# Attention two groups ahead of the routing in a gated mixture-of-experts kernel

## The reference, cut to what matters

```python
# x, ctx: 64 x 64 x 128 (4096 tokens of 128), float32
def _L0_xattn_ref(Q, K):
    scores = jnp.einsum('btd,bsd->bts', K, K)
    mask = jnp.tril(jnp.ones((Lq, Lq), dtype=scores.dtype))
    scores = scores * mask[None, :, :]
    return Q + jnp.einsum('bts,bsd->btd', scores, Q)

def _L0_ffn_ref(x, shared_w1, shared_w2, experts_w1, experts_w2, gate_w):
    shared = jnp.einsum('td,dh->th', x_flat, shared_w1.T)
    shared = jnp.einsum('th,hd->td', jax.nn.silu(shared), shared_w2.T)
    gate_logits = x_flat @ gate_w.T
    top_k_gates, top_k_idx = jax.lax.top_k(gate_logits, TOP_K)   # 2 of 8
    top_k_gates = jax.nn.softmax(top_k_gates, axis=1)
    ...
    h = jnp.einsum('td,ehd->teh', x_flat, experts_w1)            # hidden 512
    expert_out = jnp.einsum('teh,edh->ted', jax.nn.silu(h), experts_w2)
    selected = jnp.einsum('ted,te->td', expert_out, gates)
    return (shared + selected).reshape(B, S, D)

x = x + jnp.tanh(g_xattn[0]) * _L0_xattn_ref(_layernorm(x, axis=-1), ctx_1024)
x = x + jnp.tanh(g_ffn[0]) * _L0_ffn_ref(_layernorm(x, axis=-1), ...)
```

## Time and profile before

| | us |
|---|---|
| median of 3 runs | 280.01 |
| lowest, highest | 279.14, 280.99 |
| the profiled execution | 277.21 |
| its span in the profile | 275.5 |
| TensorE busy | 242.3 (88%) |
| VectorE, ScalarE, POOL busy | 127.1, 132.8, 160.1 |
| chain that ended last: TensorE, VectorE | 70%, 16% |

### The profile page before, as it was taken

The page is one execution under the profiler, slowest core; times in us unless marked ns, Lnnn a source line. Parts: engine busy times, 40 slices in busy tenths (PEclk is TensorE's granted clock), DMA queues, the critical chain, the costliest instruction groups (busy, mean ns, idle before and its releaser), DMA issues.

```text
span 275.5 us, 6308 instructions
## 1 busy us (share of the span) xinstructions
PE 242.3 (88%) x1800; PEld 213.6 (78%) x1805; DVE 127.1 (46%) x576; ACT 132.8 (48%) x293; POOL 160.1 (58%) x209
## 2 busy tenths in 40 slices
PE   8779759799799899988968799999999999999920
PEld 4466347668578577788968799999999999999920
DVE  2957969587887668811222022222110011137303
ACT  1572361637365544425543455555555655555610
POOL 5673877786764368877662465454554545555540
PEclk9977979789999999999999999999999999999985
DMA  6992111111110011775666777777776766899818
GB/s 205 399 385 78 44 51 40 48 43 39 50 42 20 20 43 45 228 183 141 193 185 176 226 221 225 203 217 221 215 217 190 234 209 201 240 272 384 337 50 295
DMA packets 32625, 46.94 MB, mean 170 GB/s; under 512 B 5472, under 2 KB 16480, under 8 KB 32336
## 3 DMA queue, kind: packets, MB, share of 16 engines
q1 hardware_dynamic: 27264, 35.45, 42.7%
q0 software_dynamic: 4320, 8.99, 9.3%
q10 hardware_dynamic: 1008, 2.10, 2.1%
HBM read 34.43 MB, written 12.09 MB: 169 GB/s over the span
## 4 chain that ended last, share of the span: by engine, by line
PE 70%; DVE 16%; issue 5%; ACT 3%; POOL 3%; DMA 2%; SPq 0%; POOLq 0%; DVEq 0%
PE bank L933 24%; PE bank L942 22%; PE bank L875 6%; PE bank L867 5%; PE bank L816 3%; PE bank L917 3%; ACT n L490 3%; PE bank L882 3%; DVE stats L570 2%; PE bank L842 2%; DMA nT<-y_rows 1%; DVE scores L605 1%; PE bank L833 1%; DVE top_at L634 1%; POOL rstd L378 1%
## 5 line engine op out<-in xcount | busy, mean ns | idle before, releaser
L452 POOL DMA_INDIRECT y_rows<-y,dest x71 | 68.9, 970 | 63.9 <-ACT y L546 59.1
L420 POOL DMA_INDIRECT expert_rows<-n,slot x64 | 63.4, 991 | 34.2 <-DVE slot L674 11.2
L933 PE MATMUL bank<-xT,w_ring 128*128 128x128 f32 x568 | 75.5, 276 | 6.5 <-issue 4.9
L933 PEld LDWEIGHTS bank<-xT,w_ring 128*128 128x128 f32 x568 | 69.0, 192 | 7.6 <-issue 5.6
L942 PE MATMUL bank<-w,hT 128*128 x568 | 74.7, 275 | 0.0
L942 PEld LDWEIGHTS bank<-w,hT 128*128 128x128 f32 x568 | 69.0, 192 | 0.0
L540 ACT ACTIVATE hT<-bank 128x512 f32<-128x512 f32 x71 | 42.4, 598 | 43.3 <-PE bank L933 42.9
L774 DVE COPY xT<-bank 128x512 f32<-128x512 f32 (+1 forms) x18 | 12.3, 684 | 101.1 <-PE bank L917 101.1
L875 PEld LDWEIGHTS bank<-sw,sT 128*128 128x128 f32 x256 | 33.3, 195 | 11.1 <-issue 11.1
L546 ACT ACTIVATE y<-bank,gate 128x128 f32<-128x128 f32 x71 | 26.1, 368 | 21.5 <-PE bank L942 21.5
L875 PE MATMUL bank<-sw,sT 128*128 128x128 f32 x256 | 34.3, 280 | 0.0
(11 more groups left out here) (124 smaller groups left out, 223.6 us busy)
## 6 DMA issues: line engine op xcount, KB each, us to landing
w_ring<-in_w1T SPq DMA_DIRECT2D x71, 256.0 KB, 3.4
x_ring<-expert_rows SPq DMA_DIRECT2D x71, 66.0 KB, 3.1
w<-in_w2T SPq DMA_DIRECT2D x2, 1024.0 KB, 15.5
kT<-y_rows SPq DMA_DIRECT2D x8, 256.0 KB, 6.3
nT<-y_rows SPq DMA_DIRECT2D x8, 256.0 KB, 4.1
out<-xres SPq DMA_DIRECT2D x8, 256.0 KB
xres<-in_xP SPq DMA_DIRECT2D x3, 512.0 KB, 10.8
kT<-in_ctxT ACTq DMA_DIRECT2D x3, 512.0 KB, 11.1
```

The lines of the kernel that those rows point to most:

```text
L420: pool.indirect_dma_start(out=x_dram[:, :], out_offset=bass.IndirectOffsetOnAxis(ap=slot[:, i, k:k + 1], axis=0), in_=n[:, i, :], in_offse ...
L452: pool.indirect_dma_start(out=y_dram[:, :], out_offset=bass.IndirectOffsetOnAxis(ap=dest[:, b:b + 1], axis=0), in_=y[:, j], in_offset=None ...
L933: last = pe.matmul(ps_up[b % UP_SLOTS][:, cols], w1_ring[:, b % W_RING, cols], xT[:, s % X_SETS, i * P:(i + 1) * P], start=True, stop=True)
```

## The change

Five things are altered.

1. *Loads.* ScalarE's queue issues only the context of groups 0 and 1. SP issues x of groups 0 and 1, waits until the latter has landed, and then issues x and context of the other groups together, with the shared weights between.
2. *Attention order.* Attention runs two to three groups ahead: in step s TensorE does `score(s+3)`, and `apply_scores(s+2)` after the logits (even s) or at the step's head (odd s). There are fewer `keep_warm` matmuls (8, 3 and 5 in place of 8, 5, 6 and 10). Units are dealt to steps by the table `UNTIL`.
3. *Roots.* `norms` works on two slots at once, in odd steps only: first and second norms of two groups in one run of 13 instructions.
4. *Logits* are read by `max` and `max_index` from PSUM, without the copy to SBUF.
5. *POOL* does a `pause()` after each of the first 40 block scatters.

```diff
-    PER_STEP = 7
+    UNTIL = (7, 14, 20, 27, 33, 40, 46, 52)
...
         def units_of(step):
-            return range((step - 1) * PER_STEP, min(UNITS * (GROUPS + 1), step * PER_STEP)) if step < GROUPS \
-                else range((GROUPS - 1) * PER_STEP, UNITS * (GROUPS + 1))
+            return range(UNTIL[step - 1] if step else 0, UNTIL[step])
...
         def _(sp):
             for i, (a, b) in enumerate(LOADS):
+                if i == 2:
+                    sp.wait_ge(x_in[1], 16)
                 sp.dma_start(xres[:, a * GW:b * GW], xP[:, a * GW:b * GW]).then_inc(x_in[i], 16)
+                if i >= 2:
+                    sp.dma_start(kT[:, a * GW:b * GW], ctxT[:, a * GW:b * GW]).then_inc(ctx_in[i], 16)
...
             norm1(0)
             norm1(1)
             routing_constants()
+            norm2(0)
             norm1(2)
-            norm2(0)
+            norm2(1)
             norm1(3)
-            norm2(1)
             block_constants()
...
+                if b < FULL:
+                    pause()
...
             act.dma_start(kT[:, 0:GW], ctxT[:, 0:GW]).then_inc(ctx_in[0], 16)
+            act.dma_start(kT[:, GW:2 * GW], ctxT[:, GW:2 * GW]).then_inc(ctx_in[1], 16)
...
             normalise(0)
+            centre_and_scale(2)
             for s in range(GROUPS):
                 evacuate_nT(s)
-                if in_range(s + 2):
-                    centre_and_scale(s + 2)
-                some = units_of(s) if s > 0 else range(0)
-                after_units(some[:PER_STEP - 2])
-                if in_range(s + 1):
-                    normalise(s + 1)
-                after_units(some[PER_STEP - 2:])
+                some = units_of(s)
+                if s % 2 == 0:
+                    if s == 0:
+                        normalise(1)
+                    if in_range(s + 3):
+                        centre_and_scale(s + 3)
+                    after_units(some[:4])
+                    if s > 0 and in_range(s + 1):
+                        normalise(s + 1)
+                else:
+                    after_units(some[:4])
+                    if in_range(s + 1):
+                        normalise(s + 1)
+                    if in_range(s + 3):
+                        centre_and_scale(s + 3)
+                after_units(some[4:])
...
-            def norms(slot, kinds):
-                out, var = rstd[:, slot, kinds], var_eps[:, slot, kinds]
-                bits, sq = half_bits[:, kinds], square[:, kinds]
+            def norms(slots, kinds):
+                out, var = rstd[:, slots, kinds], var_eps[:, slots, kinds]
+                bits, sq = half_bits[:, :, kinds], square[:, :, kinds]
...
-                dve.tensor_copy(logit[:, j], ps_logit.rearrange("p (t e) -> p t e", e=E)).then_inc(logit_read, 1)
-                dve.wait_ge(logit_read, g + 1)
                 for t in range(G):
-                    dve.max(out=top[:, g * G + t, :], in_=logit[:, j, t, :]).then_inc(top_done, 1)
+                    dve.max(out=top[:, g * G + t, :], in_=ps_logit[:, t * E:(t + 1) * E]).then_inc(top_done, 1)
...
             for_power(first(0)).then_inc(stats1_done, 1)
-            mask_scores(0)
             statistics1(1)
             for_power(first(1)).then_inc(stats1_done, 1)
+            mask_scores(0)
+            mask_scores(1)
+            residual(0)
+            for_power(second(0)).then_inc(stats2_done, 1)
             statistics1(2)
             for_power(first(2)).then_inc(stats1_done, 1)
-            residual(0)
-            for_power(second(0)).then_inc(stats2_done, 1)
-            mask_scores(1)
+            residual(1)
+            for_power(second(1)).then_inc(stats2_done, 1)
             statistics1(3)
             for_power(first(3)).then_inc(stats1_done, 1)
+            mask_scores(2)
             for s in range(GROUPS):
-                if in_range(s + 1):
-                    residual(s + 1)
-                if s == 0:
-                    for_power(second(1)).then_inc(stats2_done, 1)
-                if in_range(s + 2):
-                    mask_scores(s + 2)
-                choose(s)
-                if s > 0 and in_range(s + 3):
-                    statistics1(s + 3)
-                    norms(s + 3, slice(0, 2)).then_inc(newton, 1)
-                elif s > 0 and in_range(s + 1):
-                    norms(s + 3, slice(0, 1)).then_inc(newton, 1)
-                place(s)
+                if s % 2 == 0:
+                    choose(s)
+                    if in_range(s + 3):
+                        mask_scores(s + 3)
+                    if in_range(s + 2):
+                        residual(s + 2)
+                    place(s)
+                    for g in (s + 4, s + 5):
+                        if in_range(g):
+                            statistics1(g)
+                else:
+                    if in_range(s + 2):
+                        residual(s + 2)
+                    if in_range(s + 1):
+                        norms(slice(s + 3, s + 5), slice(0, 2) if in_range(s + 3) else slice(0, 1)).then_inc(pairs_done, 1)
+                    choose(s)
+                    if in_range(s + 3):
+                        mask_scores(s + 3)
+                    place(s)
...
             score(0)
+            score(1)
+            apply_scores(0)
+            keep_warm(3)
+            apply_scores(1)
+            score(2)
             keep_warm(5)
-            apply_scores(0)
-            score(1)
-            keep_warm(6)
             for s in range(GROUPS):
-                if in_range(s + 1):
-                    apply_scores(s + 1)
+                some = units_of(s)
+                if s % 2 == 1 and in_range(s + 2):
+                    apply_scores(s + 2)
                 transpose_n(s)
-                if in_range(s + 2):
-                    score(s + 2)
-                some = units_of(s) if s > 0 else range(0)
-                early = 0 if in_range(s + 2) else 1
-                shared_units(some[:early])
+                if in_range(s + 3):
+                    score(s + 3)
+                else:
+                    shared_units(some[:1])
                 logits(s)
-                if s == 0:
-                    keep_warm(10)
-                shared_units(some[early:4])
+                rest = some if in_range(s + 3) else some[1:]
+                if s % 2 == 0 and in_range(s + 2):
+                    apply_scores(s + 2)
+                early = 5 if s % 2 == 1 and in_range(s + 2) else 3
+                shared_units(rest[:early])
                 positions(s)
-                shared_units(some[4:6])
                 if s == GROUPS - 1:
+                    shared_units(rest[early:early + 2])
                     counts()
-                shared_units(some[6:])
-            shared_units(range((GROUPS - 1) * PER_STEP, UNITS * GROUPS))
+                    shared_units(rest[early + 2:])
+                else:
+                    shared_units(rest[early:])
+            shared_units(range(UNTIL[-1], UNITS * GROUPS))
```

23 lines of the change are left out of this document (9 added, 14 removed).

## The result

The changed kernel takes 277.1 us (median; 273.98 to 279.23), the kernel before beside it 280.01 (276.26 to 282.67). The ratio is 0.9898 [0.9862, 0.9935]: 2.9 us or 1.0% faster. Forecast were 273.0, a gain of 7.0. Medians here are of all executions, ratios of the fast ones alone (those within 1.5% of the same kernel's fastest).

A forecast was written before the change was run, and what follows sets the result against it. The prediction took the routing's hand-over to the blocks, before 118 us, as the bound. Profiled 277.21 less 7.1 gave 270.1; the median lying 2.8 us above the profiled execution, it forecast 273.0, range 268.5 to 278.

The forecast's parts named there:

- Start: First groups of the routing: choice 0 at 22.85 us, first scatter at 29.4 for 25.72, losing POOL 3.7 us.
- Roots: VectorE's inverse roots: a double run takes 3.0 us again, bounds 3.0 and 3.5; three of six runs removed.
- The walk and "7.1 us earlier" at SP: Hand-estimated routing order: last choice at 90.6 us against 98.03, SP's first block weights at 101.8, 7.1 us earlier.
- POOL fed all the way: POOL's routing scatters: never starved, last needed scatter begins at 98.9 us, 8.4 us earlier than 107.34.
- A gap of 3.7 us ahead of the blocks: TensorE before the first block rows: a new 3.7 us wait costing nothing, up to 1 us if slow clock reaches further.
- Rival (a): TensorE's clock low for longer behind both new waits: 2.5 to 5 us off the gain, 275.5 to 278; chance 0.26.
- the walk's two waits on TensorE: TensorE in the routing: waits 3.7 us for counts from 35.4 us, later 1.8 us before group 3's positions.
- Pauses at nothing: POOL's pauses after the first 40 block scatters: cost 0, a gain of up to 1 us not excluded.
- (b): The blocks gain too, as pauses let SP catch up on TensorE's 4.9 us of waits: 268 to 270; chance 0.09.
- (c): Routing not shortened: last choice at 98 us, hand-over as before, time 280; chance 0.07.
- (d): Slower: TensorE's clock low from 35 us past 70, SP 2.8 us later, time 283; chance 0.04.
- my own case: The main forecast: routing hands over to the blocks 7.1 us earlier, time 273.0 us; chance 0.54.

The follow-up runs named there:

- old_loads: The changed kernel with the loads of the kernel before; ratio to the kernel before 1.0048.
- split_roots: The changed kernel with each double run of inverse roots made as two single runs; 286.43 us, ratio to the kernel before 1.0108.
- third series: Runs with late products, among them both kernels unaltered on the first series' chip: kernel before 284.99 us, changed kernel 281.11, ratio 0.9837.
- again: The changed kernel, unaltered, measured once more; 268.97 us beside 275.47 for the kernel before, ratio 0.9748.
- before_pause: The kernel before with only the 40 POOL pauses added, in the first series; ratio to the kernel before 1.0005.
- last series: Fifth series, late products: the kernel before with the 40 pauses took 277.21 us beside 279.33 without, ratio 0.9909.
- first series: The clean series, without late products: the unaltered changed kernel took 268.97 us beside 275.47 for the kernel before, ratio 0.9748.

## Why the prediction was wrong, point by point

- **Start** (first scatter 25.72 to 29.4; choice 0 at 22.85): right, 29.25 and 22.71. That the loads may be taken at nothing was right for the sum, since the walk had them in place, but wrong as a price: old_loads puts them at 4.1 us of the first choice and 3 of the hand-over.
- **Roots, 3.0 a run, bounds 3.0 and 3.5**: right. From the first to the end of the last instruction 33.59 to 36.72, 3.1; split_roots puts three of them at 8.6 us of the hand-over.
- **The walk and "7.1 us earlier" at SP**: this term failed. It measured 1.96 in the profiled execution, was 1.66 later in the third series (110.82 against 109.16), and 7.85 earlier in the clean one, where the ratio was 0.9748 and the forecast's 273.0 to 280.01 is 0.975. The step that failed is the rule under all of it, taken from the trace before: that VectorE and ScalarE get a product when its matmul ends. In the measurement of the result they got seven products 1.1 to 3.0 us later, between 53 and 77 us, where the new order has no slack ("the choices and POOL are matched within a us"). Against `again`, choice 3 is 1.7 us later, choice 4 5.7, choice 7 6.8 and SP's first weights 7.2; two falls of the clock, at 55.5 and 69.2 us, are in this.
- **POOL fed all the way, last needed scatter at 98.9**: right when clean: the groups begin at 41.80, 53.62, 65.42, 77.22, 83.13, 89.03 and 94.93, the last needed scatter at 99.42. In the profiled execution POOL waits 6.6 us for row numbers of the later groups, and that scatter comes at 105.39.
- **A gap of 3.7 us ahead of the blocks, free but for up to 1 us**: right. It is 2.51 us in `again` and 2.23 in the profiled execution. From the first block transposes to block 30 `again` takes 72.1 us and before_pause 71.3.
- **Rival (a), clock low behind the waits**: its time, 275.5 to 278, came true by another cause, and the granted clock fell after the late products (1.91 for 1.05 us at 56.73). But the fall came behind the lateness; `again` has the walk's two waits on TensorE and the full clock, 1.00, behind both. So the rule of the Trainium skill ("TensorE: Matmul & The Clock Gate", Part 4) on transposes was not borne out as a price of these waits.
- **Pauses at nothing, a gain of up to 1 us not excluded**: right when clean (1.0005), wrong when late: 1.2% for the order before (0.9878), and 0.9% in the last series (0.9909, 2.1 us), whose kernel before (279.33) is the nearest to that of the result (280.01). I read the 2.9 us as mostly theirs, since the order before with pauses alone gained as much there; that is argued across measurements, not shown, and the 1.96 us at the hand-over would have to be lost again behind it.
- **Rivals (b), (c), (d)**: (b)'s 268 to 270 was met in the clean series (268.97), but beside a kernel before of 275.47 and by the routing, not by the blocks, so it is my own case. (c), a hand-over as before, is near to what the late series show, from another cause. (d) did not occur.

What stays open is the cause of the late products. They come with traces that hold 3453 to 3995 updates for some 6550, with both orders, in series on four chips, one of which was clean in the first series; from there to the third the kernel before grew by 9.5 us and the changed one by 12.1. Whether TensorE or only its updates are late, whether recording causes it or something else causes both, no run separates, nor why pauses on GpSimd help.

## What to carry to other kernels

Fold two runs of a chain of tiny instructions into one wherever their data can be made to wait for each other: the chain costs its length, not its width, and here three runs of some 3 us were 8.6 us of the hand-over. When the walk of an order leaves two engines matched within a microsecond, price the slack itself: a disturbance that moved the looser order's hand-over by 1.5 us moved the tight one's by 11 (the whole times by 9.5 and 12.1). And measure the parts again under other conditions before believing either: here the order had all of the gain in one condition, and in the other the pauses alone gained as much as the whole change.

## Unexpected of the hardware

- A consumer starts 0.04 to 0.14 us after the matmul's end in every clean trace, and 0.4 to 5.65 us after it for 5 to 33% of the waits in the routing of late ones. The semaphore's update is what comes late, and the delay adds up over TensorE's groups while the granted clock reads 1.00.
- The same kernel on the same chip: 275.47 and 284.99 us in two series (273.6 to 279.24 and 280.57 to 287.92).
- A pause of 0.45 us between GpSimd's scatters, on an engine with room, gave the kernel before 1.2%, 0.9% or nothing.
